# Operand places, one-source compares and PSUM banks in the two attention passes of a graph kernel

## The reference, cut to what matters

```python
# layer 0, 4 heads of 32: edges and one self loop per node
e      = leaky_relu(x_l[src] + x_r[dst], 0.2)          # per edge, 128 wide
logits = einsum('ehc,hc->eh', e, att)                  # per edge and head
p      = exp(logits - segment_max(logits, dst)[dst])
out    = segment_sum(x_l[src] * p, dst) / segment_sum(p, dst)
# layer 2, 8 heads of 16: the same with a dot product as the score
att    = sum(Q[row] * K[col], axis=-1)                 # per edge and head
out    = segment_sum(V[col] * softmax(att), row)
```

## Time and profile before

| | us |
|---|---|
| median of 3 runs | 9157.45 (9145.09 to 9171.77) |
| span of the profiled execution, first to last instruction | 7912.9 |
| median less that span | 1244.6 |

### The profile page before, as it was taken

How to read it: one execution, slowest core, us unless ns; L and a number is a source line. 1 busy time by engine, 2 the same in 40 slices (tenths; PEclk the granted TensorE clock), 3 DMA queues, 4 the chain that set the end, 5 groups by cost and what they waited for, 6 DMA issues and landing times. The chain is left out here.

```text
span 7912.9 us, 112109 instructions
## 1 busy us (share of the span) xinstructions
PE 4838.3 (61%) x32954; PEld 3963.3 (50%) x32954; DVE 4476.8 (57%) x15028; ACT 2097.8 (27%) x4735; POOL 5523.4 (70%) x5311
## 2 busy tenths in 40 slices
PE   4799887666666547777656566664555556444442
PEld 3466665566556446666635455553444444333332
DVE  9999998677777653333346666665444443111113
ACT  9454443122222241111121111112232223111110
POOL 0477777577777557777757788774777774777775
PEclk9999999788888755555577766766565558555555
DMA  0122221566666446666557766762555553333333
GB/s 15 32 56 55 53 53 35 157 162 161 158 162 160 107 87 134 134 136 134 127 149 203 205 198 200 207 197 66 156 156 156 156 156 87 99 104 104 105 104 80
DMA packets 1304014, 990.39 MB, mean 125 GB/s; under 512 B 287713, under 2 KB 1192995, under 8 KB 1303411
## 3 DMA queue, kind: packets, MB, share of 16 engines
q0 software_dynamic: 183088, 352.33, 18.0%
q1 hardware_dynamic: 700995, 378.63, 17.1%
q10 hardware_dynamic: 419328, 252.26, 11.6%
HBM read 613.75 MB, written 368.79 MB: 124 GB/s over the span
## 5 line engine op out<-in xcount | busy, mean ns | idle before, releaser
L983 POOL DMA_INDIRECT l_rows<-tab,by_src x1664 | 1813.0, 1090 | 611.0 <-issue 506.6
L983 POOL DMA_INDIRECT l_rows<-tab,by_dst x832 | 974.0, 1171 | 324.8 <-issue 237.2
L983 POOL DMA_INDIRECT l3a_rows<-tab,by_dst x832 | 804.4, 967 | 297.1 <-issue 253.3
L983 POOL DMA_INDIRECT l3b_rows<-tab,by_dst x832 | 793.5, 954 | 294.4 <-issue 253.2
L802 POOL DMA_INDIRECT sorted_dst<-pay,place_i x783 | 792.3, 1012 | 275.3 <-issue 237.8
L1129 PE MATMUL l_ps_z<-l_win,l_sel_t 128*128 128x128 f32 x3328 | 758.0, 355 | 204.6 <-DMA l_rows<-tab,by_dst 178.3
L1430 PE MATMUL l3b_ps_o<-l3b_rows,l3b_sel 128*128 128x128 f32 x1664 | 425.7, 437 | 631.3 <-DMA l3b_rows<-tab,by_dst 631.3
L1129 PEld LDWEIGHTS l_ps_z<-l_win,l_sel_t 128*128 128x128 f32 x3328 | 609.8, 251 | 227.9 <-issue 171.6
L1430 PEld LDWEIGHTS l3b_ps_o<-l3b_rows,l3b_sel 128*128 128x128 f32 x1664 | 370.5, 328 | 686.9 <-issue 686.9
L1430 PE MATMUL l3a_ps_o<-l3a_rows,l3a_sel 128*128 128x128 f32 x1664 | 402.2, 417 | 484.5 <-DMA l3a_rows<-tab,by_dst 484.5
L1457 DVE TENSOR_SCALAR l3b_sel<-iota,by_dst 128x128 f32<-128x128 f16 x832 | 186.1, 303 | 859.3 <-PE l3b_ps_o L1430 855.7
(11 more groups left out here) (423 smaller groups left out, 12349.8 us busy)
## 6 DMA issues: line engine op xcount, KB each, us to landing
parts<-l_sums ACTq DMA_DIRECT2D x416, 264.0 KB
l_win<-win SPq DMA_DIRECT2D x1664, 64.0 KB
parts<-l3a_sums SPq DMA_DIRECT2D x208, 512.0 KB, 3.0
l_row<-slot_rows ACTq DMA_DIRECT2D x624, 128.0 KB, 3.2
parts<-l_sums ACTq DMA_DIRECT2D x208, 272.0 KB, 4.0
parts<-l3b_sums SPq DMA_DIRECT2D x208, 256.0 KB, 2.4
low_bc<-lo_rows SPq DMA_DIRECT2D x194, 256.0 KB
l_rows<-tab,by_src POOLq DMA_INDIRECT x1664
```

The source lines that it names most:

```text
L983: pool.indirect_dma_start(rows[:, q, g, :], None, table, bass.IndirectOffsetOnAxis(ap=index[:, k * G + g:k * G + g + 1], axis=0))\
```

## The change

In both attention passes:

- The slot selection `sel` is made by four compares of `iota16` with one scalar per partition instead of one `tensor_tensor` compare.
- A new PSUM bank `ps_own` holds the attention vector (copied once) and `prefix`, which is no longer double-buffered. The multiplication with `att` and the backward scan read them there.
- The multiplication with the weights reads `ps_p` in PSUM instead of their copy in `val`. The copy is still made, since the sums need it, and the multiplication still waits for it. TensorE's next transpose into `ps_p` waits for the multiplication instead of the copy.
- The sums go to three buffers of one bank each; each buffer takes two tiles, so ScalarE evicts a group with two instructions of half the width.
- ScalarE, not VectorE, copies the maxima to `edge_top`, behind the exponential.

```diff
+OP = 3
-        prefix = kit.sb(f"{name}_prefix", [hg, 2, P])
-        ps_o = [kit.ps(f"{name}_ps_o{i}", [P, 2, 512]) for i in range(2)]
+        ps_o = [kit.ps(f"{name}_ps_o{i}", [P, 2 * w]) for i in range(OP)]
+        ps_own = kit.ps(f"{name}_ps_own", [P, G, P])
+        att, prefix = ps_own[:, 1], ps_own[0:hg, 2]
...
                     pe.wait_ge(exp_done, j + 1)
-                    wait_count(pe, weight_done, j)
+                    wait_count(pe, val_done, j)
                     pe.transpose(ps_p.rearrange("p g h -> p (g h)"), weight[:, j % 2], c.ident[0:hg, 0:hg])\
...
                     pe.wait_ge(val_done, j + 1)
-                    wait_count(pe, sums_done, j - 1)
-                    for g in range(G):
-                        mm = pe.matmul(ps_o[j % 2][:, g // 2, g % 2 * w:(g % 2 + 1) * w], sel[:, j % 3, g],
-                                       val[:, j % 2, g], start=True, stop=True)
-                    mm.then_inc(sums_ps, 1)
+                    for h in range(2):
+                        m = 2 * j + h
+                        wait_count(pe, sums_done, m - OP + 1)
+                        for i in range(2):
+                            mm = pe.matmul(ps_o[m % OP][:, i * w:(i + 1) * w], sel[:, j % 3, 2 * h + i],
+                                           val[:, j % 2, 2 * h + i], start=True, stop=True)
+                        mm.then_inc(sums_ps, 1)
...
                     j = k - 4
-                    act.wait_ge(sums_ps, j + 1)
                     wait_count(act, stored[j % OB], 16 * (j // OB))
-                    act.activation(sums[:, j % OB].rearrange("p (i g) w -> p i (g w)", i=2),
-                                   ps_o[j % 2][:, :, 0:2 * w], ACT.Copy).then_inc(sums_done, 1)
+                    for h in range(2):
+                        m = 2 * j + h
+                        act.wait_ge(sums_ps, m + 1)
+                        act.activation(sums[:, j % OB, 2 * h:2 * h + 2].rearrange("p g w -> p (g w)"), ps_o[m % OP],
+                                       ACT.Copy).then_inc(sums_done, 1)
...
                     act.activation(weight[:, j % 2], diff[:, j % 2], ACT.Exp).then_inc(exp_done, 1)
+                    act.activation(c.edge_top[0:hg, j], top[:, j % 2, 0::P - 1], ACT.Copy).then_inc(edge_done, 1)
...
+            if not dot:
+                dve.tensor_copy(att, c.att[:]).then_inc(homed, 1)
...
-                    dve.tensor_tensor_scan(prefix[:, j % 2], run[:, j % RB, 0:P], ps_s, -BIG, ALU.add, ALU.max)\
+                    dve.tensor_tensor_scan(prefix, run[:, j % RB, 0:P], ps_s, -BIG, ALU.add, ALU.max)\
...
                     dve.wait_ge(prefix_done, j + 1)
-                    dve.tensor_tensor_scan(top[:, j % 2, ::-1], run[:, j % RB, P:2 * P][:, ::-1], prefix[:, j % 2, ::-1], -BIG,
+                    wait_count(dve, edge_done, j - 1)
+                    dve.tensor_tensor_scan(top[:, j % 2, ::-1], run[:, j % RB, P:2 * P][:, ::-1], prefix[:, ::-1], -BIG,
                                            ALU.add, ALU.max).then_inc(top_done, 1)
...
-                                      replicate(c.att[:], 1, G), ALU.mult).then_inc(prod_done, 1)
+                                      replicate(att, 1, G), ALU.mult).then_inc(prod_done, 1)
...
-                    wait_count(dve, sums_ps, j - 2)
-                    dve.tensor_tensor(sel[:, j % 3], replicate(c.iota16[:, 0:P], 1, G),
-                                      replicate(slot[:, j * G:j * G + G], 2, P), ALU.is_equal)
+                    wait_count(dve, sums_ps, 2 * j - 4)
+                    for g in range(G):
+                        at = j * G + g
+                        dve.tensor_single_scalar(sel[:, j % 3, g], c.iota16[:, 0:P], slot[:, at:at + 1], ALU.is_equal)
...
-                                      replicate(val[:, j % 2, :, D:w], 3, width), ALU.mult).then_inc(val_done, 1)
+                                      replicate(ps_p, 3, width), ALU.mult).then_inc(val_done, 1)
...
-                if 0 <= k - 2 < GROUPS:
-                    j = k - 2
-                    dve.tensor_copy(c.edge_top[0:hg, j], top[:, j % 2, 0::P - 1])
```

More of the change, by code:

```diff
@@ L1074, in attention_pass @@
         ps_p = kit.ps(f"{name}_ps_p", [P, G, heads])
-        ps_o = [kit.ps(f"{name}_ps_o{i}", [P, 2, 512]) for i in range(2)]
+        ps_o = [kit.ps(f"{name}_ps_o{i}", [P, 2 * w]) for i in range(OP)]
+        ps_own = kit.ps(f"{name}_ps_own", [P, G, P])
+        att, prefix = ps_own[:, 1], ps_own[0:hg, 2]
         (sel_t_done, z_done, relu_done, leaky_done, prod_done, score_done, score_ps, prefix_done, top_done, diff_done, exp_done,
-         weight_ps, weight_done, val_done, sums_ps, sums_done, masks, bounds) = (
+         weight_ps, weight_done, val_done, sums_ps, sums_done, masks, bounds, homed, edge_done) = (
             kit.sem(f"{name}_{n}") for n in
@@ L1080, in attention_pass @@
              "diff_done", "exp_done", "weight_ps", "weight_done", "val_done", "sums_ps", "sums_done", "masks",
-             "bounds"))
+             "bounds", "homed", "edge_done"))
         landed, landed_before = c.pool_dma, list(c.pool_count)
@@ L1155, in _ @@
                     j = k - 5
-                    act.wait_ge(sums_done, j + 1)
+                    act.wait_ge(sums_done, 2 * j + 2)
                     act.dma_start(part_rows(c, w, j), sums[:, j % OB]).then_inc(stored[j % OB], 16)
@@ L1165, in _ @@
                     act.wait_ge(weight_ps, j + 1)
-                    wait_count(act, sums_ps, j - 1)
+                    wait_count(act, sums_ps, 2 * j - 2)
                     act.activation(val[:, j % 2, :, D:w], ps_p, ACT.Copy).then_inc(weight_done, 1)
@@ L1184, in _ @@
                 carry_masks(dve, c, key, masks)
+            if not dot:
+                dve.wait_ge(homed, 1)
             for k in range(-1, GROUPS + 4):
```

## The result

| | median of the kernel before, us | changed kernel, us | ratio (95% interval) |
|---|---|---|---|
| first result | 9156.47 (4 runs) | 9438.76 (9423.53 to 9467.84, 4 runs) | 1.0309 (1.0284 to 1.0334) |
| e9, chip 9 | 7909.94 | 7596.96 (7594.83 to 7598.65) | 0.9600 (0.9582 to 0.9618) |

The forecast was 8788 us, 4.0% less. The first result is 3.1% more, far outside the range. The second row is the same pair of kernels on another chip: there the change saves 4.0% of the time. That this is the forecast's own percentage is luck: 313 us are saved of 7910, where 369 of 9157 were forecast. Each ratio compares runs on one chip. What differs between the two rows is the subject of this part.

What follows compares the result with a forecast made beforehand. GpSimd's gathers were taken to bound both attention passes: saving 168 us in l0 and 201 in l2 cut the span from 7912.9 to 7544, and 1244.6 beyond the span made 8788 us; range 8740 to 8900, about 0.85.

Steps and rivals of the forecast that it cites:

- What bounds a pass: All passes: 832 gathers and their 0.30 us gaps fill each window, 1228 us in l0, 1261 in l2; GpSimd never stops.
- the prediction's own signs of being wrong: In the new profile: POOL gaps put down to L1233, gathers above 1.0 us ending 0.83 after a compare, l0 clock near 0.50.
- Two-source instructions hold gathers, one-source ones hardly: Attention passes: without VectorE instructions reading two SBUF tensors, 1060 us a pass, saving 168 in l0 and 201 in l2.
- the 12 us for what `sel_t` and the compares still hold: Each attention pass: remaining holds, from l1's mean gather of 968 ns, 14 ns above l3b's; 12 us a pass.
- the bound of 40: Each attention pass: upper bound on remaining holds, 832 x 0.05 = 40 us, if gathers come in phase with `sel_t`.
- VectorE's, ScalarE's and the waits' costs hidden: Attention passes: VectorE at 4.5 to 4.8 and ScalarE at 1.8 of 5.1 us a group, new waits free; cost nothing.
- The sum: Whole kernel: span 7912.9 - 369 = 7544 us, plus 1244.6 us by which the median exceeds the span, gives 8788.
- The rivals: Half clock in l0 (0.07), transfers bound l2 (0.08), change doesn't do what it says (0.03), slower (0.03).
- The clock in `l0`: Rival, chance 0.07: l0 runs at clock 0.50 throughout, taking 1310 us, total 9038; a mix gives 8850 to 9000.
- transfers: Rival, chance 0.08: transfers bound l2, sustaining only 220 GB/s, so l2 takes 1160 us and the total is 8888.
- The slower rival: Attention passes, chance 0.03: one-source compares hold gathers and two-source instructions do not; 45 us a pass more, total 9247.

Runs made afterwards that it cites:

- e9: The changed kernel, unaltered, beside the kernel before on chip 9: 7596.96 us against 7909.94, ratio 0.9600.
- e12: The changed kernel with its slot selection made by the one two-source compare again, chip 9: 7681.70 us, ratio 0.9713 to the kernel before.
- e13: The kernel before with the slot selection as four two-source compares of one tile each, chip 7: 9299.05 us, ratio 1.0010.
- e3: The kernel before with only the sums in three one-bank buffers and two half-width evictions, chip 12: 9204.53 us, ratio 1.0022.
- e1: The kernel before, unchanged, traced a second time on chip 12: 9182.94 us, with a span of 9181.2.
- e14: The changed kernel with a 128x128 GpSimd clear behind each gather of the attention passes, chip 7: 9491.43 us, ratio 1.0206 to the kernel before.
- ahead6: The changed kernel with GpSimd at most six groups ahead instead of eight: ratio 0.9589 on chip 14, 0.9595 on chip 9, 1.0221 on chip 7.

## Why the prediction was wrong, step by step

**What bounds a pass, the step that failed.** "What sets the end of a pass is how fast GpSimd gets through its gathers; the other engines wait for rows." Right for the kernel that the trace shows, and for every run on such a chip; wrong for the runs that were timed. There GpSimd already waits 190 and 107 us in the attention passes before the change, and after it 519 and 356: the gathers became as short as forecast, and `l0` longer by 187 us. It is the first of the prediction's own signs of being wrong, gaps at POOL put down to the weight multiplication. This step is why the forecast has the wrong sign.

**Two-source instructions hold gathers, one-source ones hardly.** The first half is right everywhere: 966 and 976 ns in the first result, 975 and 1022 in e9; the compares and the weights each alone, and e12 and e13 from the other side. The size was right for `l0` (saved 1228 - 1065 = 163 us, forecast 168) and too large for `l2` (1262 - 1104 = 158, forecast 201): the 12 us for what `sel_t` and the compares still hold were 57.5 in `l2`, more than the bound of 40, with the reduction and the scan in them. `l1`, from which I took the figure, has neither a reduction nor a scan.

**VectorE's, ScalarE's and the waits' costs hidden.** Right on a chip of the trace's kind: in e9 VectorE is busy for 938 of 1065 us with GpSimd's gaps intact. On the other kind e3 (1.0022) shows it for the evictions and e13 for VectorE's 0.2 us in `l0`; for the moved copy of the maxima and the single `prefix` no run takes them alone.

**The sum, which hid that step.** "The median is 1244.6 us above it, and nothing in the change touches that part, so I add it unchanged." The span of an execution ends 1.7 us before its time (9181.2 of 9182.94). The 1244.6 us were no part outside the span: trace and times came from chips on which the kernel takes 7914 and 9157 us. A gap of 14% between span and median should have been read as "this trace is not of these runs", with a range that holds both a bound by GpSimd and a bound by something else. The trace's own sum, 7544 us, lies 0.7% from the 7596.96 of e9. But with the 1244.6 us placed rightly and the bound left as it was, the forecast would still have been a gain; the bound had to be another.

**The rivals.** None of them happened. The clock in `l0` is 0.78 beside 0.80 of the unchanged kernel on such a chip; transfers have a share of 0.63 in `l2`, and in e9 they run at 231 GB/s with GpSimd never waiting for its ring beyond its gaps. The slower rival named the compares as holding gathers: side right, mechanism wrong (priced 9247, measured 9439 with short gathers). What happened is one that I didn't list: where TensorE's signals come late, the attention passes were longer in every part of the change that made their gathers shorter. Of the 282 us of the first result, beside e1, `l0` has 187 (1538 against 1351) and `l2` 79 (1407 against 1328).

**What stays open.** Why the signals come late on some chips, whether it is the rate of the gathers that makes them later (R fits most runs, not e14 in `l0`), and by what path. The trace records matmuls as finished and gives no reason for the time until the release; no run here separates a late signal from a matmul whose real end is later than its modelled one. One rival is untested: the traces with late signals are also those that lack most semaphore records, and every time here comes with a recorded span, so the recording itself may be what delays the engines.

## What to carry to other kernels

Before anything is added up, hold the profiled span against the time of the very execution: they differed by 2 us here, so a gap of a thousand means that the trace is not of these runs, and a forecast from such a trace is one for that chip only. An engine freed from being the bound is not by itself a gain: ask what the passes do when its work comes faster, and test it by putting a harmless pause in its place, with the unpaused kernel beside it on the same chip. The changed kernel is the fastest one where signals are in time (0.960, ahead6 the same), and has the highest ratio where they are late (1.031); with a pause of a 128x256 clear behind each gather it was 0.9895 there, and at that pace, 832 x 1.49 = 1240 us a pass, it would be about as fast as the kernel before on the other chips (1228 and 1262), an estimate that was not run.

## What the runs showed of the hardware

The same program takes about 7910 us on two chips and 9156 to 9297 us in the first result and on three others, with the loss in all phases, the largest part (574 us of 1268) in the sort, at a clock of 0.85 instead of 0.97 there. Where signals are late, `l2` took 1284 us with a GpSimd clear of 128x256 behind each gather and 1448 without it on the same chip; the second kernel also has the two-source compares. A GpSimd clear of 128x128 behind a gather costs 0.09 us net of its 0.24, as the 0.30 us between gathers take the rest. A gather that starts in a two-source instruction ends 0.83 us behind it (e13, as in the earlier trace rows), and with one-source compares and the other second sources in PSUM most of the hold is gone: in e9's `l0` gathers are 975 ns long instead of 1171. And a reduction from SBUF, with one source, seems to hold a gather much as `sel_t` does: 61 gathers of `l2` in e9 end 0.75 us behind it (median), for 13.3 us in all.
